# Attention, two feed-forward layers and a mixture of experts for 64 sequences: the softmax's maxima as a row of the queries

## The reference

```python
x = x + _L0_xattn_ref(ctx_2048, _layernorm(x), mask, b)    # attention over 77 keys, 8 heads of 16
x = x + _L0_ffn_ref(_layernorm(x), k0, k1, k2, s0, s1, s2) # weights of +1 and -1, 256-512-512-128
x = x + _L1_xattn_ref(_layernorm(x), ctx_2048, lens, ...)  # projection plus a gathered, decayed context
x = x + _L1_ffn_ref(_layernorm(x), W, b, Wg, bg)           # 8 experts, the best two by a softmax gate
```

```python
logits = einsum('bhqd,bhkd->bhqk', Q * depth ** -0.5, K) + b[0]
logits = logits + -1e+30 * (1.0 - mask)
weights = softmax(logits, axis=-1)
out = einsum('bhqk,bhkd->bhqd', weights, V)
```

## Time and profile before

| | |
|---|---|
| median of three runs | 530.94 us |
| lowest, highest | 530.83, 535.12 us |
| span of the profiled execution | 529.3 us, from its first to its last instruction |
| what lies around the span | 1.6 us, as median less span; no own total of the profiled execution is listed |
| TensorE busy | 489.3 us (92%), 5490 products |
| VectorE busy | 442.1 us (84%) |
| ScalarE busy | 341.8 us (65%) |
| GpSimd busy | 344.4 us (65%) |
| transfers | 28.04 MB, mean 53 GB/s |

### The profile page before, as it was taken

How to read it: one execution, slowest core, us unless ns; L and a number is a source line. 1 busy time by engine, 2 the same in 40 slices (tenths; PEclk the granted TensorE clock), 3 DMA queues, 4 the chain that set the end, 5 groups by cost and what they waited for, 6 DMA issues and landing times.

```text
span 529.3 us, 14960 instructions
## 1 busy us (share of the span) xinstructions
PE 489.3 (92%) x5490; PEld 306.4 (58%) x5490; DVE 442.1 (84%) x1428; ACT 341.8 (65%) x732; POOL 344.4 (65%) x595
## 2 busy tenths in 40 slices
PE   3677989999999999999999999999999999999976
PEld 2663576656565666656665655656565566554443
DVE  7776678888898999888898989888889876779796
ACT  2546777877768667867787566768575767754311
POOL 6448114787685769878484947669667386567762
PEclk9976999999999999999999999999999999999988
DMA  7350212013041120140403021050102000000001
GB/s 214 106 159 26 77 42 62 32 46 102 21 112 36 44 80 1 32 122 2 115 2 96 1 77 48 25 144 28 46 3 77 27 1 2 27 1 22 0 20 41
DMA packets 14193, 28.04 MB, mean 53 GB/s; under 512 B 3656, under 2 KB 5032, under 8 KB 14120
## 3 DMA queue, kind: packets, MB, share of 16 engines
q1 hardware_dynamic: 13672, 26.60, 17.3%
q10 hardware_dynamic: 448, 0.48, 0.3%
HBM read 22.80 MB, written 4.24 MB: 51 GB/s over the span
## 4 chain that ended last, share of the span: by engine, by line
PE 46%; DVE 10%; issue 3%; POOL 1%; ACT 1%; DVEq 0%; POOLq 0%
PE ps L2354 12%; PE ps L2418 12%; PE ps L2247 3%; PE ps L2299 3%; PE ps L2365 3%; PE ps L2347 2%; PE ps L2316 2%; PE ps L2385 2%; PE ps L2386 2%; DVE weighed L1207 2%; DVE h L1129 2%; PE ps L2274 1%; DVE xo L1225 1%; PE ps L2324 1%; DVE pick L1099 1%
## 5 line engine op out<-in xcount | busy, mean ns | idle before, releaser
L2418 PE MATMUL ps<-w_T,y4T 128*128 128x512 f32 x256 | 125.9, 617 | 3.5 <-DVE weighed L1207 3.3
L2354 PE MATMUL ps<-h,w 128*128 128x512 f16 x512 | 120.1, 379 | 0.5 <-DVE h L1129 0.5
L1793 ACT ACTIVATE h<-ps 128x512 f16<-128x512 f32 x128 | 74.5, 593 | 59.6 <-PE ps L2354 45.5
L1129 DVE SCALAR_TENSOR_TENSOR h<-ps,h 128x512 f16<-128x512 f32 x128 | 85.9, 681 | 15.4 <-ACT h L1793 14.1
L711 POOL TENSOR_TENSOR sum<-weighed 128x512 f32<-128x512 f32 x59 | 75.3, 1277 | 27.6 <-DVE weighed L1207 27.6
L671 POOL TENSOR_TENSOR ve<-mv,eps 128x4 f32<-128x4 f32 x64 | 14.7, 230 | 110.2 <-DVE mv L1053 110.0
L1207 DVE TENSOR_TENSOR weighed<-ps,wgt 128x1024 f32<-128x1024 f32 x59 | 71.7, 1216 | 14.7 <-PE ps L2418 14.2
L2354 PEld LDWEIGHTS ps<-h,w 128*128 128x128 f16 x512 | 47.6, 98 | 58.1 <-issue 8.6
L1759 ACT ACTIVATE prT<-ps,maskT 77x1024 f32<-77x1024 f32 x64 | 67.4, 1102 | 15.7 <-PE ps L2303 15.7
L2418 PEld LDWEIGHTS ps<-w_T,y4T 128*128 128x128 f32 x256 | 45.3, 192 | 46.6 <-issue 35.5
L676 POOL TENSOR_TENSOR rs<-ve,neg_half 128x4 f32<-128x4 f32 x64 | 65.6, 1025 | 8.6
(11 more groups left out here) (157 smaller groups left out, 929.7 us busy)
## 6 DMA issues: line engine op xcount, KB each, us to landing
cx<-in_ctx SPq DMA_DIRECT2D x16, 320.0 KB, 4.5
vx<-in_values SPq DMA_DIRECT2D x16, 320.0 KB, 4.8
kT<-in_keys SPq DMA_DIRECT2D x16, 308.0 KB, 3.3
xa<-in_x SPq DMA_DIRECT2D x16, 256.0 KB, 2.9
out_x<-xo SPq DMA_DIRECT2D x16, 256.0 KB, 2.8
plugs<-plug_d SPq DMA_DIRECT2D x16, 77.0 KB
w_T<-in_weights SPq DMA_DIRECT2D x1, 592.0 KB, 4.2
weighed<-in_weights SPq DMA_DIRECT2D x1, 592.0 KB, 5.9
```

The costliest lines, as they stand in the source:

```text
L1129: last = nc.vector.scalar_tensor_tensor(h[:, 1, (k - 1) % FC, :], src, 0.0, h[:, 0, (k - 1) % FC, :], ALU.max, ALU.subtract)
L1793: last = nc.scalar.activation(h[:, 0, (k - 1) % FC, :], src, ACT.Relu)
L2354: last = pe.matmul(pb(g, k), w2[:, i, c * 128:(c + 1) * 128], h1[:, g.p, part, i, :], start=(i == 0 and part == 0), stop=(i == FC - 1 and ...
L2418: last = pe.matmul(pm(g, j)[:, half, :], y4T[:, g.p, j * S:(j + 1) * S], w_moeT[:, half * 512:(half + 1) * 512], start=True, stop=True)
```

## The change

Groups 1 to 15 no longer subtract the maxima by `sel` products. A row of the queries carries the maximum and meets a row of -1 in the keys: in the version e of the keys the first row of the other head's 16 is -1 instead of 0 (`laid_out`). As that row has a query in it when `a_scores` runs, the maximum that VectorE finds is too low by that query; `a_row_maxima` adds it back, in two operations, and keeps fp32. For `a_weights` the row must hold the maximum instead. There are two copies of the queries for that, `qT` (its row 16 of each block is replaced, for e = 0) and `q2T` (its row 0, for e = 1). The maxima are transposed in fp32 by TensorE, copied to `mq` by ScalarE, and `spread_maxima` on SP sends them to DRAM and from there to the rows. Group 0 is computed as before. The written orders of all engines are new; in the loop the calls stand mostly within a few places of where they stood.

```diff
+        mq = sb("mq", [R * G * HR, S])
+        q2T = sb("q2T", [128, 2, W])
+        max_d = nc.dram_tensor("max_d", [2, R * G * HR, S], F32, kind="Internal").ap()
...
+        def in_rows(g):
+            return g.n >= 1
...
+            def spread_maxima(g):
+
+                sp.wait_ge(a_mT.sem, a_mT.of(g))
+                if g.has(3):
+                    sp.wait_ge(max_in[g.p].sem, max_in[g.p].of(turn(g), back=1))
+                sp.dma_start(max_d[g.p], mq[:]).then_inc(max_out.sem, 16)
+                sp.wait_ge(max_out.sem, max_out.of(g))
+                sp.wait_ge(a_q2T.sem, a_q2T.of(g))
+                for e, q in enumerate((qT, q2T)):
+                    sp.dma_start(q[HD * (1 - e)::32, g.p, :].rearrange("r (b s) -> r b s", b=G),
+                                 max_d[g.p].rearrange("(r b e) s -> e r b s", r=R, b=G)[e]).then_inc(max_in[g.p].sem, 16)
...
+            def a_row_maxima(g):
+
+                dve.wait_ge(a_max[0].sem, a_max[0].of(g))
+                dve.wait_ge(a_max[1].sem, a_max[1].of(g))
+                dve.wait_ge(a_mxT.sem, a_mxT.of(g, back=1))
+                for e in range(HR):
+                    last = nc.vector.scalar_tensor_tensor(
+                        mr[:, :, e::HR], xn[0][:, g.p, HD * (1 - e)::32].rearrange("p (b r) -> p r b", r=R),
+                        float(HD) ** -0.5, mx[:, :, e::HR], ALU.mult, ALU.add)
+                last.then_inc(a_mxs.sem, 1)
...
                 nc.scalar.activation(qT[:, g.p, :], pa(g)[:, 2, :], ACT.Copy, scale=float(HD) ** -0.5).then_inc(a_qT.sem, 1)
+                if in_rows(g):
+                    nc.scalar.activation(q2T[:, g.p, :], pa(g)[:, 2, :], ACT.Copy, scale=float(HD) ** -0.5).then_inc(a_q2T.sem, 1)
...
             def a_maxima(g):
                 act.wait_ge(a_mxT.sem, a_mxT.of(g))
+                if in_rows(g):
+                    if g.has(2):
+                        act.wait_ge(max_out.sem, max_out.of(g, back=1))
+                    nc.scalar.activation(mq[:], pa(g)[0:R * G * HR, 0, 0:S], ACT.Copy).then_inc(a_mT.sem, 1)
+                    return
...
             def a_turn_maxima(g, *readers):
                 free(*readers)
                 pe.wait_ge(a_mxs.sem, a_mxs.of(g))
+                if in_rows(g):
+                    pe.transpose(pa(g)[0:R * G * HR, 0, 0:S], mr[:].rearrange("p r i -> p (r i)"), ident[:]).then_inc(a_mxT.sem, 1)
+                    return
...
                 if q == 0:
-                    pe.wait_ge(a_mT.sem, a_mT.of(g))
-                    if g.n == 0:
+                    if in_rows(g):
+                        pe.wait_ge(max_in[g.p].sem, max_in[g.p].of(turn(g)))
+                    else:
+                        pe.wait_ge(a_mT.sem, a_mT.of(g))
                         pe.wait_ge(made_sel, 1)
...
+                        if in_rows(g):
+                            for r in range(R):
+                                rows = slice(32 * r, 32 * r + 32)
+                                last = pe.matmul(pa(g)[0:NK, r, at:at + S], kT[rows, g.p, e, b, :],
+                                                 (q2T if e else qT)[rows, g.p, b * S:(b + 1) * S], start=True, stop=True)
+                            continue
...
     for h in range(H):
+        keys[:, h, 0, 1 - h % HR] = -1.0
         keys[:, h, :, h % HR] = grouped[..., h * HD:(h + 1) * HD].transpose(0, 3, 2, 1)
```

SP's list at the start and around group 7, with the calls that it now has in this order:

```diff
+            load_rows(g[1])
+            load_keys(g[0])
             load_lens()
+            load_values(g[1])
+            load_context(g[3])
+            load_rows(g[3])
+            load_context(g[0])
+            load_context(g[1])
+            load_values(g[0])
+            load_rows(g[2])
+            load_context(g[2])
+            load_keys(g[1])
             mask_rows()
+            load_weights()
...
+            plug(g[7])
+            load_context(g[10])
             store(g[2])
+            load_keys(g[8])
+            load_values(g[8])
             load_rows(g[10])
+            spread_maxima(g[7])
```

ScalarE's list begins with `load_signs()` where it began with `mask_rows()`. TensorE's list at the start, and in the middle of a group:

```diff
             a_scores(g[0], 0)
+            count_ends()
+            a_scores(g[0], 1, (a_max[0], g[0]))
             a_turn_rows(g[1])
-            a_scores(g[0], 1, (a_max[0], g[0]))
-            count_ends((s_ends, g[0]))
+            a_scores(g[1], 0, (a_q2T, g[1]), (s_counts, g[0]))
             a_turn_maxima(g[0], (a_max[1], g[0]))
             a_weights(g[0], 0)
-            a_scores(g[1], 0, (s_counts, g[0]))
+            a_scores(g[1], 1, (a_max[0], g[1]))
+            a_turn_maxima(g[1], (a_max[1], g[1]))
             a_weights(g[0], 1, (a_prT[0], g[0]))
-            a_scores(g[1], 1, (a_max[0], g[1]))
             a_values(g[0])
-            a_turn_maxima(g[1], (a_max[1], g[1]))
-            a_turn_rows(g[2], (a_prT[1], g[0]))
+            a_weights(g[1], 0, (a_mT, g[1]))
             a_turn_out(g[0])
...
             c_turns(g[3], (c_weighed, g[2], 3))
+            a_turn_rows(g[7])
+            a_turn_maxima(g[6], (a_att, g[5]))
             b_layer(g[4], 4)
-            a_turn_rows(g[7], (a_prT[1], g[5]))
             c_project(g[3])
-            a_turn_maxima(g[6], (a_att, g[5]))
+            a_scores(g[7], 0, (a_mT, g[6]), (a_q2T, g[7]))
```

More of the change, by code:

```diff
@@ L48, in of, with __init__ @@
         return g.n * self.per + ((self.per if k is None else k) - back * self.per)
+class Later(Signal):
+    def __init__(self, signal, first):
+        self.sem, self.per, self.first = signal.sem, signal.per, first
+    def of(self, g, k=None, back=0):
+        return super().of(g, k, back) - self.first * self.per
 class Norm:
@@ L475, in plug @@
             def plug(g):
-                if g.n == 0:
+                if not g.has(2):
                     sp.wait_ge(plug_out, 32)
@@ L579, in _ @@
             store(g[7])
+            load_keys(g[13])
             load_values(g[13])
+            load_rows(g[15])
+            spread_maxima(g[12])
+            plug(g[13])
+            store(g[8])
+            load_keys(g[14])
             load_values(g[14])
-            load_keys(g[14])
-            store(g[8])
-            load_values(g[15])
+            spread_maxima(g[13])
+            plug(g[14])
             store(g[9])
             load_keys(g[15])
-            plug(g[13])
+            load_values(g[15])
+            spread_maxima(g[14])
+            plug(g[15])
             store(g[10])
-            plug(g[14])
+            spread_maxima(g[15])
             store(g[11])
-            plug(g[15])
             store(g[12])
@@ L1417, in _ @@
             a_highest(g[8], 1)
-            a_split_maxima(g[8])
+            a_row_maxima(g[8])
             d_gates(g[4])
@@ L2142, in _ @@
             c_turned(g[11])
+            a_maxima(g[14])
+            a_queries(g[15])
             b_high(g[12], 4)
-            a_queries(g[15])
-            a_maxima(g[14])
+            b_normalise(g[13])
             b_high(g[12], 5)
```

915 lines of the change are left out of this document (456 added, 459 removed).

## The result

The changed kernel takes 543.02 us (median of five runs, 539.73 to 543.88), the kernel before 530.94: ratio 1.0204, 95% interval 1.0163 to 1.0246. It is 2% slower. The prediction, 529.4 with a range to 539.0, was wrong. In later sets a few executions took over 1.5% longer than the fastest of their kernel; the medians and ratios here leave those out.

The account below looks back on a forecast made before the run. TensorE was taken as the bound after a start of dependent chains. The sum was 530.9 + 7 (start) - 9.2 (products removed) + 0.7 (transposition) = 529.4 us, with a range of 521.5 to 539.

Parts of the forecast that it names:

- Products removed: TensorE's `a_weights` without the subtracting products: 0.66 us saved a group, 9.2 us over groups 2 to 15 (6.7 to 10.4).
- Transposition of the maxima: On TensorE, one fp32 transposition at 0.11 us replaces a bf16 product at 0.06: +0.05 a group, 0.7 us over 14.
- VectorE: Two operations on the maxima replace four, relieving VectorE by 0.6 to 0.9 us a group; taken as 0, up to -3 us.
- ScalarE's second copy: In `a_queries`, a second copy of 0.596 us, 15 times; taken as 0, or 8.3 us if its cover were gone.
- The two transfers: SP's write and reads of the maxima take some 6 us within a 13.3 us gap; taken as 0, 7 us left.
- The start: SP's mask rows queue behind more loads and land at 17 us, making the first scores 7 us late (4.6 to 8).
- The chain after the first scores: From the first scores to `b_turns(g[0])`, 33.2 us: length taken as unchanged (-3 to +4), so the whole +7 survives.
- The orders: New call orders in the dense part and at the end were taken to keep about the same work: 0.
- The second: Rival: VectorE becomes the bound in the dense stretch and nothing of the 9.2 us comes back: 538.6 us; chance 0.12.
- my own case: The whole kernel: start delay, products saved and transposition added give 529.4 us; chance 0.58.
- The third: Rival: SP issues the maxima's transfers late, behind waiting loads and a store; 8 us late gives 543; chance 0.08.
- The first: Rival: the mask rows do not wait at the start, so the dense saving stands alone: 522.4 us; chance 0.22.

Follow-up runs that it names:

- e8: e5 with the rows of groups 7 and 12 issued ahead of a spread and the last maxima copied earlier on ScalarE; 522.84 us, ratio 0.9848.
- e2: The changed kernel's orders with the old subtracting products, the maxima split in four operations and no transfers of the maxima; 552.76 us, ratio 1.0370.
- e5: e3 with nearly every spread ahead of the waiting row load, a few key loads ahead of a spread, group 15's maxima turned earlier; 530.75 us, ratio 0.9996.
- e3: The new mechanism in the orders of the kernel before, each spread of the maxima behind the row load three groups on; 535.71 us, ratio 1.0087.
- e4: The kernel before with its first 15 loads in the changed kernel's order and the signs ahead of ScalarE's mask rows; 542.61 us, ratio 1.0199.
- e7: The changed kernel with SP's starting loads as before, except contexts 2 and 3 ahead of the counts, and the signs last; 540.48 us, ratio 1.0171.
- e9: The changed kernel with the chain before the gates' transpositions moved ahead on GpSimd, ScalarE and VectorE, TensorE's order unchanged; 594.04 us, ratio 1.1164.
- e12: The changed kernel with TensorE's order around the gates' transpositions put back as before in nine groups; 541.23 us, ratio 1.0194.
- e6: The changed kernel with mask rows issued early, and TensorE's gate calls and the experts' first call each one call later; 562.58 us, ratio 1.0550.
- e10: The changed kernel with the loads and every engine's calls up to the first group's second LayerNorm in the old order; 537.59 us, ratio 1.0083.
- e11: e10 with ScalarE's squares for groups 2 and 3 and group 0's decays moved behind the second half of group 1's weights; 538.14 us, ratio 1.0134.

## Why the prediction was wrong

**Products removed: right in kind, too large.** I took 0.66 us a group, 9.2 in all; a half is 0.27 shorter, so 0.54 a group, 7.6 over 14, nearer the lower bound of 6.7 than my choice. The row of `a_values` was the wrong neighbour: its 32 records take 0.95 us, the new half 1.05. The estimate from the Trainium skill, "TensorE: Matmul & The Clock Gate", sections "Wait — 56ns, not 53.3ns?" and "Why this matters for your kernels", had been 0.58 a group; the measurement is nearer to it than to my choice.

**Transposition of the maxima: right** (0.12 against 0.11).

**VectorE: right at the helpful end.** Two operations, 0.18 us each in the median, take the place of four, and in the old orders TensorE's idle time between att(3) and att(15) falls from 6.5 us in before to 3.8 in e8. Its waits for VectorE there fall from 6.0 to 3.3 us; I had 0 to -3.

**ScalarE's second copy: right for the dense stretch.** It is 0.592 us fifteen times, and the wait for `xn` is 11.8 us without it (e2) and 11.9 with it. In the start, where I let it vanish in a chain of unchanged length, TensorE waits 1.4 us for it.

**The two transfers: right for after, by its order.** SP's places are good there. The 7 us of slack are real but not for free: where a spread stood behind a waiting load, or a load behind a waiting spread, e5 was 7.9 and e3 12.9 us slower than e8, which has them mended.

**The start: the mechanism was right, the size was not. This is the term that failed most.** I took +7; it is +12.45 at the first scores and +12.2 at group 3. My landing at 17 us stood for 3.7 MB at 285 GB/s, between two stretches of the earlier trace rows, one of them with a hole in it and one in another phase. SP's two mask rows take 11.4 and 13.0 us from their issues at 8.88 and 9.4, so they land between 20 and 22.5. From 4 to 21.1 us (8.88 + 12.2) 4.1 MB moved, at 242 GB/s: 309 in the first four us, 220 from 8 to 20. So the rate was too high, and the amount too low as well, because a part of the weights, issued behind the mask rows, moved before these had landed. With my 3.7 MB the true mean gives a landing at 19.3. That 3.7 MB at 220 GB/s would give 20.8 is in part luck. My upper bound, 17.8 us, was no bound: it came from the slower of the two rates, and nothing had excluded one below both. The Trainium skill, "DMA: Bandwidth & Descriptors", section "Queues, rings and completion order", says that each DMA engine consumes descriptors in ring order; SP's mask rows agree, 9.6 KB in 12.2 us. Order in one queue is not the whole of it: ScalarE's two mask rows, issued at 6.42 and 7.0 us in its own queue, where only the signs (landed by 5.7) and 1.5 KB of scales stood ahead, took 8.8 and 9.6 us; in before the median is 3.3. So the backlog of SP's queue delayed small transfers of another queue too. e4 shows that the loads' order is worth 11.5 us of the span by itself in the orders of before.

**The chain after the first scores: right in number, 34.3 us against 33.2.** That it is right is partly luck. The reason given, that what follows depends on the scores step by step, did not hold in the new orders. In e7 the scores begin at 10.70, and att(0) comes 34.6 us after them; in after it is 27.7, in before 23.3. There the chain hangs on contexts and on ScalarE's squares as well, so 7.3 of the 12.2 us stay when the loads are put right. After has the clock on its side besides: 1.00 in its first 50 us, 0.85 in before.

**The orders: the step that I did not take.** "The new orders keep about the same work in it" and, of the end, "keeps its operations and nearly their order" was all that I said of them: I priced the mechanism and the start and no other move. With the same mechanism, e8 against after, the orders cost 12.4 us up to att(3) (114.78 - 102.39) and 9.5 in the twelve groups, and give back 3.1 in the end: 18.8 in all, the whole distance of the two spans (518.8, 537.6). Of that, 9.5 - 3.1 = 6.4 us stand in none of my terms.

With the measured sizes the sum is 529.3 + 12.2 - 7.6 + 0.7 + 6.4 = 541.0 for a span of 537.6. The 3.4 us that are too many are mostly VectorE's relief in e8 (2.7), against which the 6.4 were taken. So two terms carry the miss in the span: the start, 5.2 us too small, and the orders of the dense part, put at nothing.

**The clock: no term of mine.** The median execution of after has a span of 541.0 us at 0.973, 3.4 us above the profiled one. The profiles of e9 and e12, which have the orders of after until past att(3), show where such time goes: att(3) at 117.20 and 117.03 us instead of 114.78, at a grant of 0.59 from 36 to 48 us and 0.61 from 56 to 72. By them 2.3 of the 3.4 us are lost in the start, and against the start of before, whose trace also has the lower level in it, the loss is 14.5 us. The rest of the 3.4 is not placed.

**Rivals.** The second gave 538.6, nearer than my own case, for a reason that is not there: TensorE's idle time from 99 to 495 us is 10.0, where it asked for well above 15; and a group takes TensorE 29.9 us (358.8 / 12), not 32. The third is real as a mechanism, but after is not its case; that its example, 8 us of lateness, gives 543, the measured number, is chance. The first did not occur. My remark that the order at the end was what I passed over, if all steps held, named the wrong part: the end is shorter, the middle has lost.

**What is not settled.** Which move in the new orders opens the wait for `xn`, and what holds the twelve groups at 359 us. Three attempts to close it, from TensorE's side (e6, e12) and from the others' (e9), moved it or made it worse; e12 took most of it away there and gained nothing. In the start, what stays without the loads is not put down to single calls: e10 has the loads and the calls of before and still reaches att(3) at 110.81, e11 at 111.42. No execution of after itself was profiled at the lower clock.

## What to carry to other kernels

Judge a mechanism and an order apart: here the same change is worth 1.5% in the old orders, mended at a few places, and costs 2% in new ones. When many loads are put ahead of a small one that the first product needs, count the bytes on all queues, some of those behind it too, and take a low rate: the one measured with the queues full at that place of the program. Compare traces at like clocks, and read the trace of a kernel that shares the stretch where its own is the exception. A wait in a list that is busy most of the time is not removed by moving its two ends; measure what the call that takes its place then delays.

## What the runs showed of the hardware

With the queues full of transfers of 256 to 448 KB, the sixteen DMA engines moved 220 GB/s at a share of 1.06 from 8 to 20 us, in e2 and e4, with the same loads, 231 and 216; in before, 351 GB/s at 0.97. So the share does not tell the rate; why the rate is low there is open.

Executions of the same program differ by 5 to 7 us together with the mean granted clock: e7 534.84 us at 0.997, and 540.07 to 541.50 at 0.973 to 0.979. The mean does not order them by itself: e8 took 523.32 us at 1.000 and 520.79 at 0.991. In the traces of before, after, e2 and e8 the grant is 1.00 throughout the dense stretch; the low level stands in the start and, in before, near the end (0.94 from 480 to 529 us). The same calls can get either level there. The stretch from 36 to 48 us of after and of e12, whose lists are the same up to there:

```profile
36.00:48.00 12.00, 8.46 (x146) 7.23 (x147) 9.70 (x33) 5.08 (x14) 10.59 (x19) 1.00 0.33 95
```

```profile
36.00:48.00 12.00, 8.71 (x152) 7.61 (x152) 9.45 (x32) 6.19 (x14) 10.51 (x18) 0.59 0.32 95
```

In the four us before, TensorE was busy 3.20 us in after and 2.95 in e12. In e10 and e11 att(0) came 1.5 to 2.3 us earlier than in before, and att(1) 8 us later, at a granted clock of 0.66 and 0.62; how much of the 8 us is the clock was not separated.
